# First attention: decay folded into scaled q and k, scores computed a second time in transposed form with the maximum subtracted in the product

## The reference, cut to what matters

```python
q = x @ W_q
k = x @ W_k
v = x @ W_v
latent_kv = (k + v) @ W_down_kv
k_rec = (latent_kv @ W_up_k).reshape(b, s, H, HD).transpose(0, 2, 1, 3)
v_rec = (latent_kv @ W_up_v).reshape(b, s, H, HD).transpose(0, 2, 1, 3)
...
scores = jnp.einsum('bhqd,bhkd->bhqk', qh, k_rec) / math.sqrt(d)
decay = jnp.exp(-LAMBDA_DECAY * jnp.abs(t[:, None] - t[None, :]))
scores = scores * decay[None, None, :, :]
attn = jax.nn.softmax(scores, axis=-1)
out = jnp.einsum('bhqk,bhkd->bhqd', attn, v_rec)
...
return out @ W_o
```

## Time and profile before

| | us |
|---|---|
| median of 3 runs | 3765.04 (3763.25 to 3765.86) |
| span of the profiled execution | 3759.3 |
| of it projections, up to the first DMA of the heads | 142.5 |
| of it heads | 1065.1 (142.5 to 1207.6) |
| of it output | 44.9 (1207.6 to 1252.5) |

### The profile page before, as it was taken

The page is one execution under the profiler, slowest core; times in us unless marked ns, Lnnn a source line. Parts: engine busy times, 40 slices in busy tenths (PEclk is TensorE's granted clock), DMA queues, the critical chain, the costliest instruction groups (busy, mean ns, idle before and its releaser), DMA issues. The chain is left out here.

```text
span 3759.3 us, 71272 instructions
## 1 busy us (share of the span) xinstructions
PE 3174.3 (84%) x21288; PEld 2152.6 (57%) x21288; DVE 2380.3 (63%) x5292; ACT 2097.1 (56%) x3482; POOL 844.5 (22%) x1652
## 2 busy tenths in 40 slices
PE   6699999999999639996883599959688888797879
PEld 3366666666666339996441499944355555533433
DVE  4488888888886664444567644435477677435853
ACT  3589989898987224442221344422266666354544
POOL 2211111111110114443001244524422222120112
PEclk9899999999999769998896799979899899898889
DMA  3300000000000314433003244331211111100001
GB/s 116 101 22 25 25 25 22 25 25 25 22 24 16 113 52 90 90 79 74 9 0 113 66 92 91 73 81 62 83 51 51 47 52 52 24 0 12 0 18 39
DMA packets 148659, 186.76 MB, mean 50 GB/s; under 512 B 20304, under 2 KB 114768, under 8 KB 148560
## 3 DMA queue, kind: packets, MB, share of 16 engines
q1 hardware_dynamic: 123984, 151.94, 12.6%
q0 software_dynamic: 24576, 33.57, 5.5%
HBM read 122.54 MB, written 62.91 MB: 49 GB/s over the span
## 5 line engine op out<-in xcount | busy, mean ns | idle before, releaser
L1717 DVE CUSTOM_DVE_ANT_0 s0Ah_SD<-s0Ah_ps_s,s0Ah_table 128x1024 f32<-128x1024 f32 x512 | 623.3, 1218 | 40.1 <-PE s0Ah_ps_s L1808 25.2
L1763 ACT ACTIVATE s0Ah_PM<-s0Ah_SD,s0Ah_nb 128x1024 f32<-128x1024 f32 x512 | 594.6, 1161 | 24.6 <-POOL s0Ah_nb L1706 24.6
L1818 PEld LDWEIGHTS s0Ah_ps_t<-top_ident,s0Ah_PM 128*128 128x128 f32 x4096 | 480.8, 141 | 103.0 <-ACT s0Ah_PM L1763 3.4
L1818 PE MATMUL s0Ah_ps_t<-top_ident,s0Ah_PM 128*128 128x128 f32 x4096 | 533.8, 273 | 0.4
L1769 ACT COPY s0Ah_PT<-s0Ah_ps_t 128x512 f32<-128x512 f32 x512 | 302.9, 592 | 104.3 <-PE s0Ah_ps_t L1818 99.8
L2021 ACT ACTIVATE s4Ch_PM<-s4Ch_SD,s4Ch_nb 128x260 f32<-128x260 f32 (+2 forms) x512 | 254.3, 497 | 145.7 <-POOL s4Ch_nb L1964 132.3
L1808 PE MATMUL s0Ah_ps_s<-s0Ah_ks,s0Ah_qs 96*128 96x512 bf16 x1024 | 308.5, 383 | 28.2 <-DMA s0Ah_ks<-s0A_parts 27.5
L1725 DVE COPY s0Ah_PT<-s0Ah_ps_t 128x512 f32<-128x512 f32 x384 | 264.9, 690 | 94.7 <-PE s0Ah_ps_t L1818 91.9
L1706 POOL TENSOR_TENSOR s0Ah_nb<-s0Ah_mx,s0Ah_minus 128x1 f32<-128x1 f32 x512 | 98.2, 192 | 930.5 <-DVE s0Ah_mx L1717 930.5
L1831 PE MATMUL s0Ah_ps_v<-s0Ah_PT,s0Ah_Vs 128*32 128x512 f32 x2048 | 273.9, 607 | 0.0
L1975 DVE CUSTOM_DVE_ANT_0 s4Ch_SD<-s4Ch_ps_s,s4Ch_table 128x260 f32<-128x260 f32 (+2 forms) x512 | 205.1, 408 | 79.8 <-PE s4Ch_ps_s L2066 65.2
(11 more groups left out here) (389 smaller groups left out, 7432.8 us busy)
## 6 DMA issues: line engine op xcount, KB each, us to landing
s1M_raw_w<-in_L_ffn_w SPq DMA_DIRECT2D x16, 1024.0 KB
s3M_raw_w<-in_L_ffn_w SPq DMA_DIRECT2D x16, 1024.0 KB
s0A_parts<-s0Ap_sp SPq DMA_DIRECT2D x48, 256.0 KB, 2.4
s4C_parts<-s4Cp_sp SPq DMA_DIRECT2D x48, 256.0 KB, 2.4
s0Ah_qs<-s0A_parts SPq DMA_DIRECT2D x64, 96.0 KB
s0Ah_ks<-s0A_parts SPq DMA_DIRECT2D x64, 96.0 KB
s4Ch_qs<-s4C_parts SPq DMA_DIRECT2D x64, 96.0 KB
s4Ch_ks<-s4C_parts SPq DMA_DIRECT2D x64, 96.0 KB
```

The source lines that it names most:

```text
L1717: nc.vector.tensor_tensor_reduce(SD[u % NBUF][:, :], ps_s[u % 2][:, :, :].rearrange("p a n -> p (a n)"), table[:, (TB - 1 - t) * P:(TB - 1 ...
L1763: nc.scalar.activation(PM[u % NBUF][:, :], SD[u % NBUF][:, :], ACT.Exp, bias=nb[:, u:u + 1]).then_inc(e_ok, 1)
L1818: x = nc.tensor.transpose(ps_t[:, bank, k * P:(k + 1) * P], PM[u % NBUF][:, at:at + P], ident[:, :])
```

## The change

**Projections.** `SplitSets` takes the place of `Split`. VectorE multiplies q and k, as they come out of PSUM, each by two tables along the token axis (`falls`, exp(-0.01 t) with scale, and `grows`, its inverse): four sets of 128 x 1024 in each group instead of two copies by ScalarE. Each set is written as an fp32r top and an fp32r rest (ScalarE casts the top; VectorE forms the rest of two sets, GpSimd of two), eight DMAs of 512 KB in each group instead of six of 256 KB. The copies of v move from VectorE to ScalarE. The loops are written out.

**Heads.** All 512 units are written out, with no loop. For a unit i:

- `score`: two fp32r matmuls with a contraction of 48 rows (top, top and rest against top, rest and top). The two heads of a pair stand on rows 0 to 47 and 64 to 111 of the array, as tiles of 64 rows; in each step of TensorE's program the scores ahead take one of the two tiles and `shifted` takes the other.
- VectorE does only the product with the table and the maximum (L1717 before). The table now undoes the scaling where the sign is wrong, and is 1 elsewhere. GpSimd subtracts the maximum from the 128 x 128 block on the diagonal (`DG`).
- `turned`, `negated`, `rest_of`: once in a pair the 128 x 16 maxima are transposed, ScalarE negates them and GpSimd forms the rest; then SP copies them by eight DMAs (`maxima`) into rows 48 and 49 of q, beside rows of ones in k.
- `shifted`: the scores again, with keys on the partitions and queries as columns, contraction 50 rows; the product holds the score minus the maximum. Queries after the key tile take the set `plus`, those before it the set `minus`; a half of 512 columns that holds the diagonal is one or two matmuls of 384 columns together, and `diagonal` transposes the block `DG` into the gap.
- `exps`: ScalarE, two exponentials of 512 columns from PSUM into `PM`, which is then the operand of `values` as it stands. The eight transposes of a unit, the copies of `ps_t`, and `gathered` are gone.
- `values`: four fp32 matmuls of 512 columns and 17 columns of values for each key tile of a pair, summed over the eight key tiles in PSUM; ScalarE copies the result out once in a pair and SP stores it to `OD` in DRAM.

TensorE's scores run 24 units ahead of `shifted`, since the maxima of a pair have to be known first. `shifted` of a pair's first unit waits for the pair's eight maxima DMAs (`rows_in`).

**Output.** `project_heads` takes the place of `project_out` for this stage: it loads the sums and the results from `OD` (32 DMAs of 128 KB), forms reciprocals as fp32r top and rest, spreads them with a 0/1 matrix on TensorE (32 fp32r matmuls), multiplies on VectorE, and applies W_o.

```diff
+                for k, (ps, table) in enumerate(((ps_q, falls), (ps_q, grows), (ps_k, grows), (ps_k, falls))):
+                    split.before_f(dve, g, k)
+                    dve.wait_ge(q_mm if k < 2 else k_mm, START + g + 1)
+                    nc.vector.tensor_tensor(split.F[k][:, :, :], ps[:, :, :],
+                                            table[:, h * GT:(h + 1) * GT].unsqueeze(1).to_broadcast([P, DC, GT]),
+                                            ALU.mult).then_inc(split.f_ok, 1)
...
+    NP = B * H // 2
+    U = 2 * TB
+    AHEAD = U + 8
+    TURN = AHEAD - U - 2
+    NPB, NSD, NX = 12, 3, 3
...
+            def maxima(p):
+                sp.wait_ge(nr_ok, START + p + 1)
+                for r in range(2):
+                    for n in range(2):
+                        for q in (plus[p % 3][0], minus[p % 2][0]):
+                            z = r * 64 + SROW + n
+                            sp.dma_start(q[z:z + 1, :].bitcast(F32).rearrange("a (t q) -> a t q", t=TB),
+                                         NMp[p % 2][n][r * TB:(r + 1) * TB, :].bitcast(F32)).then_inc(rows_in[p % 2], 16)
...
+            for p in range(NP):
+                if p >= 1:
+                    sp.wait_ge(x_mm, START + use_of(p * U - 1, 1) + 1)
+                if p + 2 < NP:
+                    load(p + 2, 0, plus[(p + 2) % 3], plus_in[(p + 2) % 3])
+                if p + 1 < NP:
+                    load(p + 1, 1, minus[(p + 1) % 2], minus_in[(p + 1) % 2])
+                if p >= 1:
+                    store(p - 1)
+                if p + 1 < NP:
+                    maxima(p + 1)
...
+            def rest_of(p):
+                pool.wait_ge(e_ok, START + turn_use(p) + 1)
+                nc.gpsimd.tensor_tensor(NMp[p % 2][1][:, :], NM[:, :], NMp[p % 2][0][:, :].bitcast(F32),
+                                        ALU.subtract).then_inc(nr_ok, 1)
+            for i in range(N):
+                p, t, r = i // U, i % U // 2, 1 - i % 2
+                pool.wait_ge(m_ok, START + i + 1)
+                nc.gpsimd.tensor_tensor(DG[p % 3][:, r * TB + t, :], SD[i % NSD][:, t * P:(t + 1) * P],
+                                        mx[p % 3][:, r * TB + t:r * TB + t + 1].to_broadcast([P, P]),
+                                        ALU.subtract).then_inc(dg_ok, 1)
+                if i % U == 4 and p:
+                    rest_of(p - 1)
+            rest_of(NP - 1)
...
-            def copy(i, u):
-                dve.wait_ge(ta_mm, START + i + 1)
-                q = u % G * P
-                nc.vector.tensor_copy(PT[u // G % 2][:, 0:G, q:q + P],
-                                      ps_t[:, 0, :].rearrange("p (k q) -> p k q", k=G)).then_inc(ta_ok, 1)
...
+            def negated(p):
+                u = turn_use(p)
+                act.wait_ge(x_mm, START + u + 1)
+                if p >= 2:
+                    act.wait_ge(rows_in[p % 2], ROWS * (p // 2))
+                if p:
+                    act.wait_ge(nr_ok, START + p)
+                nc.scalar.activation(NMp[p % 2][0][:, :], ps_x[u % NX][0:U, 0:P], ACT.Copy, scale=-1.0)
+                nc.scalar.activation(NM[:, :], ps_x[u % NX][0:U, 0:P], ACT.Copy, scale=-1.0).then_inc(e_ok, 1)
+
+            def exps(i):
+                for half in range(2):
+                    u, n = use_of(i, half), 2 * i + half
+                    act.wait_ge(x_mm, START + u + 1)
+                    if n >= NPB:
+                        act.wait_ge(pv_mm, START + (n - NPB) // 4 + 1)
+                    nc.scalar.activation(PM[n % NPB][:, :], ps_x[u % NX][:, :], ACT.Exp).then_inc(e_ok, 1)
+
+            def collect(p):
+                act.wait_ge(pv_mm, START + (p + 1) * TB)
+                if p >= 2:
+                    act.wait_ge(out_to[p % 2], 16 * (p // 2))
+                nc.scalar.copy(OE[p % 2][:, :], ps_v[:, :]).then_inc(ov_ok, 1)
...
+            def score(i, half):
+                p, t, r = i // U, i % U // 2, 1 - i % 2
+                q, k = plus[p % 3]
+                if half == 0:
+                    if i % U == 0:
+                        pe.wait_ge(plus_in[p % 3], LOADS * (p // 3 + 1))
+                    if i >= 2:
+                        pe.wait_ge(m_ok, START + i - 1)
+                x = nc.tensor.matmul(ps_s[i % 2][:, half, :], q[at(r), t * P:(t + 1) * P],
+                                     k[at(r), half * GT:(half + 1) * GT], start=True, stop=True)
+                if half == 1:
+                    x.then_inc(s_mm, 1)
+
...
+            def shifted(i, half):
+                p, t, r = i // U, i % U // 2, i % 2
+                u = use_of(i, half)
+                if half == 0 and i % U == 0:
+                    pe.wait_ge(minus_in[p % 2], LOADS * (p // 2 + 1))
+                    pe.wait_ge(rows_in[p % 2], ROWS * (p // 2 + 1))
+                if u >= NX:
+                    pe.wait_ge(e_ok, START + u + 1 - NX)
+                bank = ps_x[u % NX]
+                cut = min(max(t - half * G, 0), G) * P
+                after = min(max(t + 1 - half * G, 0), G) * P
+                for (q, k), lo, hi in ((minus[p % 2], 0, cut), (plus[p % 3], after, GT)):
+                    if lo < hi:
+                        x = nc.tensor.matmul(bank[:, lo:hi], k[with_m(r), t * P:(t + 1) * P],
+                                             q[with_m(r), half * GT + lo:half * GT + hi], start=True, stop=True)
+                if cut == after:
+                    x.then_inc(x_mm, 1)
+
+            def diagonal(i):
+                p, t, r = i // U, i % U // 2, i % 2
+                u = use_of(i, t // G)
+                pe.wait_ge(dg_ok, START + p * U + 2 * t + 2 - r)
+                nc.tensor.transpose(ps_x[u % NX][:, t % G * P:(t % G + 1) * P], DG[p % 3][:, r * TB + t, :],
+                                    ident[:, :]).then_inc(x_mm, 1)
+
+            def values(p, t):
                 for r in range(2):
...
+                    n = 2 * p + r
+                    for half in range(2):
+                        j, w = 2 * r + half, 4 * (p * TB + t) + 2 * r + half
+                        pe.wait_ge(e_ok, START + use_of(2 * (p * TB + t) + r, half) + 1)
+                        if t == 0:
+                            pe.wait_ge(ov_ok, START + p)
+                        x = nc.tensor.matmul(ps_v[j * 32:j * 32 + HD + 1, :], V[:, n // H, n % H, t, :],
+                                             PM[w % NPB][:, :], start=(t == 0), stop=(t == TB - 1),
+                                             tile_position=(0, j * 32))
+                x.then_inc(pv_mm, 1)
...
+            for i in range(N):
+                ahead = i + AHEAD
+                if (i + TURN) % U == 0 and (i + TURN) // U < NP:
+                    turned((i + TURN) // U)
+                diag = i % U // 2 // G
+                for half in range(2):
+                    if ahead < N:
+                        score(ahead, half)
+                    shifted(i, half)
+                    if half == diag and diag == 0:
+                        diagonal(i)
+                if diag == 1:
+                    diagonal(i)
+                if i % 2 == 1 and i >= 3:
+                    values((i - 3) // U, (i - 3) % U // 2)
```

## The result

The changed kernel takes 3947.78 us (median of 4 runs, 3942.43 to 3952.09) against 3765.28 us: 1.0496 times as long (95% interval 1.0480 to 1.0512), 182.5 us slower where 93 us less had been forecast.

A forecast was written before the change was run, and what follows sets the result against it. TensorE was taken to bound the heads before and after. From 3759.3 us, heads -100, projections +4 and output +3 gave 3666 us, or 3672 with the 5.7 us around it; range 3570 to 3850 us.

The forecast's parts named there:

- The clock: Heads: behind each pair's wait TensorE runs briefly at the lower clock, losing 1.4 us a pair (bounds 0 and 1.7).
- The wait for the maxima: Heads, each pair's first `shifted`: TensorE waits 2.7 us for the maxima's DMAs, a chain of 8.7 us against 6.2 of cover.
- The unit: Heads: TensorE needs 1.55 us for a unit of 128 keys, against 2.04 before.
- The start of the heads: Before the first `shifted`: about 11.5 us of loads, then 24 units of scores alone at VectorE's pace, 27.5 us.
- The bound on ScalarE and VectorE: Heads: VectorE needs 1.15 us a unit and ScalarE about 1.0, so neither reaches what TensorE needs.
- Projections: Projections stretch: 33.6 MB of writes at about 330 GB/s, 102 us; +4 us, between -3 and +15.
- Output: Output stretch: transposes go, 32 spreading matmuls and a wait for loads come; +3 us, between -5 and +12.
- The rivals: Cheaper weights and changes (3575 us, 0.13), row tiles apart (3845, 0.14), values' passes laddered (3878, 0.12), long maxima chain (3765, 0.07).

The follow-up runs named there:

- e9: Changed kernel with scores 26 units ahead, maxima's rest two units earlier, fourth `plus` buffer, and two-part loads each split in two: 3521.92 us, 0.938 of the kernel before.
- e3: Kernel before the change, with TensorE made to wait for three small DMAs once in each pair of heads: 3889.46 us, 1.035 of the kernel before.
- e7: Changed kernel with the values' matmuls taking 32 columns of weights instead of 17 in seven of eight key tiles: 3926.2 us, 1.044 of the kernel before.
- e4: Changed kernel without the diagonal block's transposes, its shifted scores formed from `plus` (outputs differ there): 3734.94 us, 0.993 of the kernel before.
- e12: Changed kernel with two whole-array bf16 matmuls added to every unit, splitting its first score and shifted matmul: 4590.51 us, 1.222 of the kernel before.
- e15: Changed kernel with eight whole-array bf16 matmuls directly ahead of each diagonal transpose, results overwritten: 3830.96 us, 1.019 of the kernel before.
- e11: Changed kernel with only the loads spread over all DMA engines: two executions, 3850.38 and 3946.68 us.
- e5: Changed kernel with scores 26 units ahead, maxima's rest two units earlier, and a fourth `plus` buffer loaded one pair earlier: 3726.33 us, 0.992 of the kernel before.

## Why the prediction was wrong, step by step

- **The clock: the step that failed.** "A gap of 2.7 us every 25 us is near that. Bounds are 0 and 1.7 us a pair; I take 1.4." The heads of the changed kernel are 427 us longer than those of e9 (1246.9 and 819.9). The waits make 104 of them (the row of L1914 above), so some 320 us go to the lower clock, about 10 us a pair, six times the upper bound. The stretches say the same: 754 us at the lower clock behind the start, at 5.25 us for two units instead of 3.02, lose 320 us by this estimate. The rows were right for the work that stood behind the gaps there, and e3 confirms them for the old heads (1.3 us a gap). I carried them over to work that uses 48 and 50 rows of the array and changes shape five or six times in two units, and gave them a bound that no row of such work had set.
- **The wait for the maxima: mis-sized.** 3.45 us instead of 2.7. The single-row DMAs follow each other 0.69 us apart, not 0.46 (662.28 to 667.09 for seven steps), which is 1.6 us more; the four units of cover are 4 x 0.14 = 0.6 us shorter, as a unit is faster than counted; so the rest of the chain was over-counted by some 1.2 us. It stood inside the bound of 2.0 to 3.5.
- **The unit: right within 5%.** 1.41 us in the rows above, 1.51 in the most frequent pattern of e9 (3.02 us for two units), 1.47 on average there, against 1.55. The forecast's heads without wait and clock are 965 - 127 = 838 us; e9 has 820. That they are so near is in part two errors that cancel: 512 x 0.08 = 41 us less for the units, 23 us more for a start that takes 10 us longer and for units at the lower clock behind it. Row tiles side by side, eight passes of values in one microsecond and VectorE well below its limit were all as foreseen.
- **The start of the heads: mis-sized.** 11.5 us of loads and 27.5 us of scores alone were counted, 39 us. From 136.7 us on it takes 18.2 us to the first score and 53.8 to the first shifted one, with a wait of 4.2 us for the first maxima that no term had: 15 us more, and all of it at the lower clock.

```profile
154.85 1.23 PE L1889 MATMUL s0Ah_ps_s<-s0Ah_plus_k,s0Ah_plus_q 48*128 48x512 f32 x4 [31.94 <-DMA s0Ah_minus_k<-s0Ah_ones]
190.51 0.66 PE L1914 MATMUL s0Ah_ps_x<-s0Ah_plus_q,s0Ah_plus_k 50*128 50x384 f32 x1 [4.21 <-DMA s0Ah_minus_q<-s0Ah_NM_rest]
```

- **The bound on ScalarE and VectorE: right.** VectorE is busy 622 of 1247 us, ScalarE 609; in e9, with TensorE at its fastest, 611 and 564 of 820.
- **Projections:** -5.8 us, just outside the -3 to +15. Between 40 us and the end the DMAs moved 344 GB/s at a share of 0.93, so more than the 330 I had worked out, and the last write was issued at 129.6 us.
- **Output:** +10 us instead of +3, inside its bounds. VectorE waits 2.67 us in each group for `OT`, whose four loads of 128 KB come every 5.15 us (102 GB/s): loads of four heads, again with a small outermost size.

```profile
1406.28 1.28 DVE L2282 TENSOR_TENSOR s0Ao_OT<-s0Ao_OT,s0Ao_ps_b 128x512 f32<-128x512 f32 x2 [2.67 <-DMA s0Ao_OT<-s0A_OD]
```

- **The rivals.** Of the four none happened. What did is the forecast's own course with one term six times larger than its bound, for which there was no rival. The row that would have asked for one is the earlier trace rows itself: it showed that the clock reacts within microseconds, and the earlier trace rows showed a kernel that had nearly no gap to react to. A rival "the pair's wait costs the clock for most of a pair", with 10 us a pair in place of 1.4, would have given 31 x 8.6 = 267 us more, 3672 + 267 = 3939 us; but its 10 us are known from the result alone.

Two things stay open. One is whether columns matter as rows do: e7 moved the columns and shows too little to tell. The other is what brings the clock back: rows, changes of tile shape and the place in the pair move together in e4, e12 and e15, and e11 had short and long stretches with the same units.

## What to carry to other kernels

A short wait on TensorE is not priced by its length alone, but by the work behind it too: in this kernel, whose work uses 48 and 50 rows of the array and changes its tile shape five or six times in two units, a wait of 3.45 us put the next 24 us at the lower clock, and taking the last waits away gave a jump, not a share (1022 to 820 us of heads). In the old kernel a wait of 2.7 us cost 3.4 us at that clock. And look at the outermost size of each DMA: from e5 to e9 two loads of 16 rows took the place of one of 2 x 16, and with that went the last waits.

## What was not expected of the hardware

- TensorE busy without a pause on 48-row matmuls for 3.5 us lost its clock as if idle (0.70 and 0.72 over the heads); with 96 or 128 rows it did not (0.89, 0.87).
- Added useless matmuls on the whole array, some 0.46 us to each unit of 1.41, made the kernel 3% faster (3948 to 3831 us).
- In e12 the clock fell 3.4 us after it had come back with TensorE busy all the time, and stayed down for 47.8 us; so a mixture of work can lose the clock without any wait.
- Single-row DMAs out of SBUF take 0.69 us from issue to issue on SP, the short ones of 16 rows 0.46.
- While the loads with 2 as their outermost step drained, 2.4 of 16 DMA engines were busy; with each of them split in two the pair's loads no longer delayed anything.
